# Second expert layer of a two-layer network: three sorted parts instead of two, another order of DMA issues, pairs combined by ScalarE and TensorE

## The reference, cut to what matters

```python
scores = softmax(xt @ gate_w.T)                       # 8 experts
idx = top_k(scores + gate_b, 2)                       # two experts for each token
cw = sum(one_hot(idx) * scores[idx])                  # their weights
h1 = xt @ w1.T + b1;  h3 = xt @ w3.T + b3             # for each expert, 256 columns
a = swiglu(h1 * h3)      # g = min(even, 7); l = clip(odd, -7, 7); g * sigmoid(1.702 g) * (l + 1)
routed = sum_e cw[e] * (a @ w2[e].T + b2[e])
shared = swiglu((xt @ sw1.T + sb1) * (xt @ sw3.T + sb3)) @ sw2.T + sb2     # a ninth expert, for all tokens
x = x + gb * (routed + shared)
```

## Time and profile before

| quantity | value |
|---|---|
| median of three runs | 1788.88 us |
| device time of the profiled execution | 1786.69 us |
| its span, first to last instruction | 1784.9 us |
| TensorE busy over the span | 80% |
| VectorE, ScalarE, GpSimd busy | 74%, 51%, 35% |
| mean granted TensorE clock | 0.886 of full speed |
| 1496 to 1553 us | norm, router, sort positions |
| 1553 to 1589 us | 11 shared blocks |
| 1598 to 1725 us | 46 routed blocks |
| 1725 to 1745 us | the last 5 shared blocks |
| 1745 to 1785 us | TensorE idle; gather, combine, store |

### The profile page before, as it was taken

How to read it: one execution, slowest core, us unless ns; L and a number is a source line. 1 busy time by engine, 2 the same in 40 slices (tenths; PEclk the granted TensorE clock), 3 DMA queues, 4 the chain that set the end, 5 groups by cost and what they waited for, 6 DMA issues and landing times. The chain is left out here.

```text
span 1784.9 us, 41566 instructions
## 1 busy us (share of the span) xinstructions
PE 1429.1 (80%) x15014; PEld 979.8 (55%) x15014; DVE 1327.3 (74%) x3609; ACT 909.5 (51%) x2099; POOL 617.2 (35%) x586
## 2 busy tenths in 40 slices
PE   1267767776749758999999999999999983779990
PEld 0167767766744324555555555555555553658870
DVE  5699999999577855666676666667667667658886
ACT  1455555555321023666666666666666651336760
POOL 3396667665012232611111111111111003275346
PEclk7678888888859969999999999999999996689995
DMA  1310000000000001211111111111111000028962
GB/s 72 98 38 2 1 1 1 1 1 1 7 6 1 10 10 20 42 27 26 26 29 31 30 30 31 30 31 29 29 31 32 8 10 14 11 95 229 249 176 88
DMA packets 146373, 71.53 MB, mean 40 GB/s; under 512 B 95219, under 2 KB 131589, under 8 KB 146053
## 3 DMA queue, kind: packets, MB, share of 16 engines
q1 hardware_dynamic: 141508, 60.62, 15.3%
q0 software_dynamic: 4096, 8.40, 1.6%
q10 hardware_dynamic: 576, 0.07, 0.0%
HBM read 38.11 MB, written 18.35 MB: 32 GB/s over the span
## 5 line engine op out<-in xcount | busy, mean ns | idle before, releaser
L1178 DVE TENSOR_REDUCE ntop<-score 128x1 f32<-128x512 f32 x512 | 318.0, 683 | 253.0 <-PE score L1059 253.0
L1137 ACT ACTIVATE prob<-score,ntop 128x512 f32<-128x512 f32 x512 | 317.6, 687 | 270.1 <-DVE ntop L1178 270.1
L391 ACT ACTIVATE hist<-zp 128x168 f32<-128x168 f32 (+1 forms) x768 | 224.1, 313 | 171.3 <-DVE zp L359 170.6
L1095 PE MATMUL turned<-ident,prob 128*128 128x128 f32 x2048 | 268.6, 280 | 1.4 <-DVE probT L1121 1.4
L441 PEld LDWEIGHTS py<-hist,diagC 128*128 128x128 f32 x2048 | 260.3, 212 | 0.0
L441 PE MATMUL py<-hist,diagC 128*128 128x128 f32 x2048 | 260.0, 295 | 0.0
L1059 PE MATMUL score<-ks,qs 64*128 64x512 f32 x1024 | 257.2, 621 | 0.0
L1095 PEld LDWEIGHTS turned<-ident,prob 128*128 128x128 f32 x2048 | 218.9, 141 | 49.2 <-issue 28.5
L411 POOL TENSOR_TENSOR xb<-xc,Bm 128x1024 f32<-128x1024 f32 x128 | 244.7, 1948 | 1.3
L354 DVE TENSOR_TENSOR gp<-hist,Ap 128x168 f32<-128x168 f32 (+1 forms) x768 | 231.0, 331 | 14.6 <-POOL xb L411 14.6
L359 DVE TENSOR_TENSOR zp<-gp,xb 128x168 f32<-128x168 f32 (+1 forms) x768 | 234.7, 336 | 0.0
(11 more groups left out here) (293 smaller groups left out, 1571.6 us busy)
## 6 DMA issues: line engine op xcount, KB each, us to landing
w<-in_ew SPq DMA_DIRECT2D x46, 320.0 KB, 3.8
tb<-in_table SPq DMA_DIRECT2D x64, 127.1 KB
sorted_h<-nought SPq DMA_DIRECT2D x2, 2944.0 KB, 17.1
xs<-sorted_h SPq DMA_DIRECT2D x46, 128.0 KB
sorted_y<-ysb SPq DMA_DIRECT2D x46, 128.0 KB
rel_q<-q_sb SPq DMA_DIRECT2D x256, 8.0 KB
ks<-k_sb SPq DMA_DIRECT2D x32, 128.0 KB
key_q<-q_sb SPq DMA_DIRECT2D x248, 8.0 KB
```

Source lines behind the costliest of these rows:

```text
L391: nc.scalar.activation(hist[:, par, u, lo:hi], zp[j][:, 0:hi - lo], ACT.Tanh)\
L1095: last = nc.tensor.transpose(turned_ps[BANK[e]][:, j * P:(j + 1) * P], prob[G % 2][e][:, j * P:(j + 1) * P], ident[:, :])
L1137: nc.scalar.activation(prob[G % 2][e][:, :], score_ps[r][:, :], ACT.Exp, bias=ntop[:, G % 2, e:e + 1]).then_inc(prob_ready, 1)
L1178: v.tensor_reduce(ntop[:, G % 2, e:e + 1], score_ps[r][:, :], AX.X, ALU.max, negate=True)\
```

## The change

- The tokens are sorted in three parts of 1024, 2048 and 1024 tokens. The padding of 7 blocks is now paid three times: 15, 23 and 15 blocks, 53 instead of 46.
- `ORDER` is now 8 shared blocks, the 15 routed ones of part 0, 2 shared blocks, the 38 routed ones of parts 1 and 2, and 6 shared ones.
- SyncE's program is written in another order: five loads of weights and four of slots ahead of the loop, then for each block m `load_weights(m + 5)`, `store(m)`, `load_slots(m + 4)`. `store` no longer lags five blocks.
- The product with b2 leaves the shared blocks. It is done at the very end, in TensorE's sum of the pairs: ScalarE multiplies each gathered row by its weight (64 ACTIVATEs of 128 columns), TensorE adds b2's product and the two rows in PSUM (32 times one 9-row product and two products with the identity), and VectorE adds the PSUM bank to `acc` in `finish`.
- The biases of the routed blocks are picked by four small TensorE products instead of VectorE's multiply and reduce.
- The counting of positions works in quarters of 1024 tokens; some small VectorE operations are added and some removed.

```diff
-PARTS = 2
-RB = 2 * PT * P // SLOTS + NE1 - 1
+QT = 8
+PART_QUARTERS = (1, 2, 1)
+PT = [QT * q for q in PART_QUARTERS]
+RB = [2 * t * P // SLOTS + NE1 - 1 for t in PT]
...
-    NW, NX, NY, NGOT = 5, 4, 4, 8
-    AFTER = NW
-    ORDER = ([("shared", i) for i in range(SHARED_FIRST)] + [("routed", m) for m in range(NROUTED)]
-             + [("shared", i) for i in range(SHARED_FIRST, NSHARED)])
+    NW, NX, NY, NGOT = 5, 4, 4, 4
+    SHARED_FIRST, SHARED_THEN = 8, 2
+    ORDER = (shared(0, SHARED_FIRST) + routed(0, RB[0]) + shared(SHARED_FIRST, SHARED_FIRST + SHARED_THEN)
+             + routed(RB[0], NROUTED) + shared(SHARED_FIRST + SHARED_THEN, NSHARED))
...
-            load_slots(0)
-            for m in range(NROUTED):
-                if m + 1 < NROUTED:
-                    load_slots(m + 1)
-                load_weights(m)
-                if m >= AFTER:
-                    store(m - AFTER)
-            for m in range(NROUTED - AFTER, NROUTED):
-                store(m)
+            for m in range(NW):
+                load_weights(m)
+            for m in range(NX):
+                load_slots(m)
+            for m in range(NROUTED):
+                if m + NW < NROUTED:
+                    load_weights(m + NW)
+                store(m)
+                if m + NX < NROUTED:
+                    load_slots(m + NX)
...
+            for k in range(NT):
+                act.wait_ge(got_in[k % NGOT], 32 * ring(k, NGOT))
+                for r in range(2):
+                    A.activation(got[:, 2 * k + r, :], got[:, 2 * k + r, :], ACT.Copy, scale=wt[:, r, k:k + 1])\
+                     .then_inc(weighted, 1)
...
-                    if kind == "shared":
-                        k = i * HALVES + o
-                        mm(Y[n % 2][:, cols], cwT[:, k * P:(k + 1) * P], b2[:, :], start=True, stop=False)
...
+            for j in range(NBLK):
+                if SUMS_IN[j] == 6:
+                    pe.wait_ge(y_taken, N)
+                for q in range(TPB):
+                    k = j * TPB + q
+                    bank = pm[SUMS_IN[j]][:, q * P:(q + 1) * P]
+                    mm(bank, cwT[:, k * P:(k + 1) * P], b2[:, :], start=True, stop=False)
+                    for r in range(2):
+                        pe.wait_ge(weighted, 2 * k + r + 1)
+                        last = mm(bank, ident[:, :], got[:, 2 * k + r, :], start=False, stop=(r == 1))
+                last.then_inc(summed, 1)
```

More of the change, by code:

```diff
@@ L34 @@
 ALPHA = 1.702
-PARTS = 2
-PT = NT // PARTS
 SLOTS = 2 * P
@@ L41 @@
 NSHARED = NB * SEQ // SLOTS
-RB = 2 * PT * P // SLOTS + NE1 - 1
-NROUTED = PARTS * RB
-MOST = PT * P // SLOTS
+QT = 8
+QUARTERS = NT // QT
+PART_QUARTERS = (1, 2, 1)
+PARTS = len(PART_QUARTERS)
+PT = [QT * q for q in PART_QUARTERS]
+T0 = [sum(PT[:s]) for s in range(PARTS + 1)]
+RB = [2 * t * P // SLOTS + NE1 - 1 for t in PT]
+R0 = [sum(RB[:s]) for s in range(PARTS + 1)]
+NROUTED = R0[PARTS]
+MOST = max(PT) * P // SLOTS
+PART_OF = [s for s in range(PARTS) for _ in range(RB[s])]
 class Chain:
@@ L1267, in experts1 @@
     WCOLS = 5 * P
-    NW, NX, NY, NGOT = 5, 4, 4, 8
+    NW, NX, NY, NGOT = 5, 4, 4, 4
     N = NSHARED + NROUTED
-    AFTER = NW
-    SHARED_FIRST, SELECT_AT, IN_LOOP, EVERY = 11, 4, 8, 2
-    ORDER = ([("shared", i) for i in range(SHARED_FIRST)] + [("routed", m) for m in range(NROUTED)]
-             + [("shared", i) for i in range(SHARED_FIRST, NSHARED)])
+    SHARED_FIRST, SHARED_THEN = 8, 2
+    SELECT_AT = 2
+    shared = lambda lo, hi: [("shared", i) for i in range(lo, hi)]
+    routed = lambda lo, hi: [("routed", m) for m in range(lo, hi)]
+    ORDER = (shared(0, SHARED_FIRST) + routed(0, RB[0]) + shared(SHARED_FIRST, SHARED_FIRST + SHARED_THEN)
+             + routed(RB[0], NROUTED) + shared(SHARED_FIRST + SHARED_THEN, NSHARED))
     place_of = {b: n for n, b in enumerate(ORDER)}
@@ L1305, in experts1 @@
         chosen = sb("chosen", [P, NT, NE1])
-        upto = [sb(f"upto{i}", [P, PARTS, PT + 1, NE1]) for i in range(2)]
+        upto = [sb(f"upto{i}", [P, QUARTERS, QT, NE1]) for i in range(2)]
         top = sb("top1", [P, NT])
@@ L1362, in bias @@
         def bias(n, c):
-            kind, i = ORDER[n]
-            return ball[:, NE1, c:c + 1] if kind == "shared" else bsel[:, i, c:c + 1]
+            kind, m = ORDER[n]
+            return b1_shared[:, c:c + 1] if kind == "shared" else b1_sel[:, c, m:m + 1]
         @block.sync
@@ L1424, in _ @@
             for s in range(PARTS):
-                for k in range(s * PT, (s + 1) * PT):
+                for k in range(T0[s], T0[s + 1]):
                     for r in range(2):
@@ L1430, in _ @@
                 for i in range(NY):
-                    pool.wait_ge(y_out[i], 16 * stores(i, (s + 1) * RB))
-                for k in range(s * PT, (s + 1) * PT):
+                    pool.wait_ge(y_out[i], 16 * stores(i, R0[s + 1]))
+                for k in range(T0[s], T0[s + 1]):
                     if k >= NGOT:
@@ L1611, in join @@
                  .then_inc(a_ready, 1)
[L1613 to L1618, removed]
             def finish(j):
                 ts = slice(j * TPB, (j + 1) * TPB)
+                dve.wait_ge(summed, j + 1)
+                chain(v.tensor_tensor(acc[:, ts, :], acc[:, ts, :],
+                                      pm[SUMS_IN[j]][:, :].rearrange("p (q e) -> p q e", q=TPB), ALU.add))
                 chain(v.tensor_tensor(acc[:, ts, :], acc[:, ts, :],
@@ L1638, in _ @@
                     lins(n)
[L1639 to L1645, removed]
-                    combine(k)
-                if k % TPB == TPB - 1:
-                    finish(k // TPB)
+            dve.wait_ge(y_taken, N)
+            for j in range(NBLK):
+                finish(j)
         @block.tensor
@@ L1723, in down, with select @@
                     cols = slice(o * P, (o + 1) * P)
-                    if kind == "shared":
-                        k = i * HALVES + o
-                        mm(Y[n % 2][:, cols], cwT[:, k * P:(k + 1) * P], b2[:, :], start=True, stop=False)
-                    last = mm(Y[n % 2][:, cols], a[:, n % 2, cols], w[:, 4 * P:5 * P],
-                              start=(kind == "routed"), stop=True)
-                last.then_inc(y_ready, 1)
+                    last = mm(Y[n % 2][:, cols], a[:, n % 2, cols], w[:, 4 * P:5 * P], start=True, stop=True)
+                last.then_inc(y_ready, 1)
+            def select():
+                pe.wait_ge(eid_ready, 2)
+                for c in range(4):
+                    last = mm(XT[0][:, c * NROUTED:(c + 1) * NROUTED],
+                              b1_rows[:, :].rearrange("e (p c) -> e c p", c=4)[:, c, :], mine[:, :],
+                              start=True, stop=True)
+                last.then_inc(spots_ps, 1)
             for n in range(N + 2):
+                if n == SELECT_AT:
+                    select()
+                if n + 1 == SHARED_FIRST:
+                    pe.wait_ge(sel_ready, 1)
                 if n + 1 < N and ORDER[n + 1][0] == "routed":
```

143 lines of the change are left out of this document (73 added, 70 removed).

## The result

The changed kernel takes 2124.9 us (median of four runs, 2123.8 to 2129.2), the one before 1788.5 beside it: ratio 1.189, 95% interval 1.1875 to 1.1905. 2081 was forecast, 1965 to 2135 given as the range. The profiled execution has a span of 2122.4 us against 1784.9. Until the 16th scatter the two traces are level (first scatter at 1552.7 and 1551.8); all of the difference lies behind it.

A forecast was written before the change was run, and what follows sets the result against it. Bound by a chain: scatters, routed blocks (TensorE and SyncE's queue nearly level), gathers, last sum. First `turn` 1577.9 + 11.6 + 45 steps 414.0 + 14.6 + 17.0 + 33.6 + 2.1 + 6.1: span 2076.9, forecast 2081 us, range 1965 to 2135.

The forecast's parts named there:

- The circle: Routed blocks: slots queued behind `store`, which waits for the block just ended, so `turn` waits in 45 steps of 9.2 us.
- The start: First routed `turn` after part 0's scatters: at 1577.9 instead of 1598.3, 20.4 us earlier.
- The step: One waiting routed block: TensorE 4.2, SyncE's queue 2.0, slots' landing 3.0, together 9.2 us, bounds 6.7 and 10.3.
- The queue: SyncE in a routed step, from the end of `down` to the issue of the slots: 2.01 us.
- The landing: Routed step, from the issue of the slots to `turn`: 3.0 us, bounds 2.26 and 3.4.
- TensorE's part of the step: One routed block's work, starting at half clock after a pause of 5 us: 4.2 us, bounds 2.44 and 4.88.
- Rival 1: Every waiting routed block wholly at half clock: 4.88 us of work, a step of 9.9, 2112 us; chance 0.25.
- Rival 2: Routed blocks at full clock in spite of the pauses: a step of 7.45 us, 2002 to 1967 us; chance 0.20.
- The sum of pairs: TensorE's products at the kernel's end: 1.05 us for each of 32 tiles at full clock, 33.6 us in all.
- rival 4: Final sum of pairs at half clock, or held up by ScalarE: 33.6 us more, 2115 us; chance 0.04.
- close of the span: Kernel's end, from VectorE's last sum to the end of the span: 6.1 us.
- Rival 3: Routed blocks without a wait for slots, at SyncE's pace of 2.57 us: 1784 us, faster by 5; chance 0.06.

## Why the prediction was right

- **The circle.** Right, place and count: 45 waits at `turn`, as counted from the order of SyncE's queue. Undone alone it gives back 311 of 336 us; put alone into the kernel before it gives steps of 9.0 to 10.3 us there. Of the prediction's readings one is off: in the earlier trace rows the run of nines is slices 17 to 32, not 22 to 34, and the second experts begin in slice 34. Nothing in the sum rests on it.
- **The start.** 1577.9 forecast, 1576.9 measured.
- **The step, 9.2 forecast.** The last 33 steps (1716.2 to 2033.8) average 9.62. The queue took 1.60 us instead of 2.01: the register load takes 0.26 us here, not the 0.68 of the earlier trace rows; why is not shown. The landing took 3.16 us in the step shown (2.1 to 3.9 over all, median 3.2) for 3.0, nearer to my bound of 3.4, for slots that land in turn behind the weights, than to 2.26. The Trainium skill (DMA: Bandwidth & Descriptors, Queues, rings and completion order) has each DMA engine take its descriptors in ring order. The trace agrees as far as it goes: weights issued at 1857.33 and slots at 1858.22 take about 3.2 us each to land; slots that overtake the weights would have had to land in 2.3 us.
- **TensorE's part of the step, 4.2 forecast.** It was 4.73 on average (4.97 in the step shown): of the step's three terms this is the one mis-sized upwards most. I took 4.2 from the one pause in the earlier trace rows, where the clock rose 3.6 us into the work behind it. Here it rises from 2.8 to 5.7 us after a block's first product, or not at all before the next block, so one pause was too few to set it by. What fixes the moment is not shown. Rival 1, every block wholly at half clock, holds for 23 of the 43 blocks. The Trainium skill (TensorE: Matmul & The Clock Gate, HAM oscillation) tells of tiles whose work is shorter than the wait for their data and which all start at half clock. The trace agrees for 44 of the 45 waits: 2.44 us of work at full clock against waits of 4.6 to 5.7 us, and every block starts at half clock; the 45th wait is 3.14 us, and the clock is full behind it. Rival 2 (full clock) was wrong in fact, and its arithmetic right: 7.45 forecast, 7.5 on average with the pauses filled.
- **The sum of pairs, 33.6 forecast, 60.2 measured.** Mis-sized, by 26.6 us, more than the steps. I gave rival 4 a chance of 0.04, since "TensorE works without a break there". The trace has it busy without a break, and the clock stayed at half all the same. So the step of the prediction that failed here is that busy means full clock. The price of a change of depth, which I had from the earlier trace rows (0.20 us), was about right: 0.19 us with the products grouped.
- **What hid in the total.** Start of the sum 2057.6 for 2035.1 (+22.5), the sum +26.6, close of the span 2.5 us after the last sum instead of 6.1 (-3.6): +45.5, the whole difference of the spans (2122.4 - 2076.9). Why the close is shorter is not shown: in both traces the last store is issued 0.03 us after the last sum. The range held because it was wide. Nearest to 2125 are rival 4 (2115) and rival 1 (2112), each given as if the other did not happen; both happened, in part, and priced in full together they come to 2146, outside the range.
- **Rival 3** (no wait at the slots) set 1784 us. With the wait gone the kernel took 1813.9. The wrong term was the sum at full clock, some 26 of the 30 us.

## What to carry to other kernels

For each load in an in-order queue, count how many steps lie between the wait that stands ahead of it and the step that wants its data; free buffers do not help a load that stands behind a wait for the step just ended. When such a wait opens on TensorE, price it twice, as itself and as the half clock of the work behind it. And give products of few rows a place beside their like, or pad them: between products of full depth they cost a change each time (0.2 us here), and in this kernel's sum the clock too.

## What the runs showed of the hardware that I had not expected

- TensorE recorded busy for 58 of 58 us stayed at half clock when 9-row products and 128-row ones alternated, one to two. With the same products grouped four and eight, or padded to 128 rows, it was at full clock. The clock fell early in all these sums. With the products grouped or padded it came back (fallen at 1750.4 and 1749.0, back at 1753.8 and 1752.4); where they alternated it did not. In the shared blocks of the kernel before, 9-row and 128-row products alternate as well, beside four full ones of 256 columns, at full clock. What makes the difference between the two places is not settled here.
- Added useless work made the kernel 95 us faster, by keeping the clock at full.
- With the same wait and the same block each time, the clock rose anywhere from 2.8 to 5.7 us after a block's first product, or not before the next block.
- The kernel before took 5% longer on another chip. In the traces of its variants from there ScalarE's instructions were 7 to 22 us apart from about 1575 to 1641 us, while the scatters ran, with no instruction of the kernel shown as what they waited for; behind the scatters they were normal. What held them was not found.
